# Pairwise attention on one Trainium2 core: the 28 second slots of a tile all on ScalarE, and the copies of the transposed probabilities split one to three

## The reference, cut to what matters

```python
def _L1_gnn_ref(feat, adj, W1, W2, a):
    mask = jnp.where(adj > 0, 0.0, NEG_INF)
    q = feat @ W1.T
    k = feat @ W2.T
    e = jax.nn.relu(q[:, None, :, :] + k[:, :, None, :])   # every pair of nodes, 64 features
    scores = jnp.einsum('bijd,d->bij', e, a)
    att = jax.nn.softmax(scores + mask, axis=-1)
    return att @ feat
```

## Time and profile before

| | us |
|---|---|
| median of 3 runs (12303.48 to 12307.22) | 12305.15 |
| the profiled execution | 12303.05 |
| its span, first to last instruction | 12301.3 |
| PE busy in the span | 11965.8 (97%) |
| DVE busy | 10281.1 (84%) |
| ACT busy | 9346.4 (76%) |
| L611, slots on ScalarE, 3328 of them | 6398.1 |
| L881, first slots on VectorE, 4096 of them | 5252.8 |
| L1359, matmuls of the slots, 61440 | 6739.6 |

### The profile page before, as it was taken

How to read it: one execution, slowest core, us unless ns; L and a number is a source line. 1 busy time by engine, 2 the same in 40 slices (tenths; PEclk the granted TensorE clock), 3 DMA queues, 4 the chain that set the end, 5 groups by cost and what they waited for, 6 DMA issues and landing times.

```text
span 12301.3 us, 239883 instructions
## 1 busy us (share of the span) xinstructions
PE 11965.8 (97%) x106113; PEld 5936.3 (48%) x106113; DVE 10281.1 (84%) x12373; ACT 9346.4 (76%) x7633; POOL 458.4 (4%) x636
## 2 busy tenths in 40 slices
PE   7999999999999999999999999999999999999999
PEld 3333853338433384333843348433484334843348
DVE  4999849998599975999759997599975999759997
ACT  3898739987499874988748887489874898749986
POOL 1000000000000000000000000000000000000000
PEclk9999999999999999999999999999999999999999
DMA  2000320003200031000310003100031000310003
GB/s 74 19 21 22 105 80 22 18 22 113 76 18 18 24 117 69 18 18 26 125 59 18 18 27 132 52 18 18 31 137 43 18 22 29 140 38 19 21 32 106
DMA packets 206087, 609.72 MB, mean 50 GB/s; under 512 B 45440, under 2 KB 137216, under 8 KB 139520
## 3 DMA queue, kind: packets, MB, share of 16 engines
q1 hardware_dynamic: 184176, 450.72, 10.5%
q0 software_dynamic: 20880, 143.66, 3.1%
HBM read 556.47 MB, written 8.39 MB: 46 GB/s over the span
## 4 chain that ended last, share of the span: by engine, by line
DVE 52%; PE 45%; issue 1%; ACT 0%; SPq 0%; DMA 0%; POOL 0%; DVEq 0%
DVE E L881 34%; PE ps L1339 10%; DVE E L889 9%; PE ps L1443 8%; PE ps L1359 7%; PE ps L1456 4%; PE ps L1516 4%; PE ps L1423 4%; PE ps L1372 4%; DVE T L904 2%; PE ps L1502 2%; DVE E L879 1%; DVE HW L915 1%; DVE adj_ring L896 1%; PE ps L1322 1%
## 5 line engine op out<-in xcount | busy, mean ns | idle before, releaser
L611 ACT ACTIVATE E<-QB,KBP 128x2048 f32<-128x2048 f32 x3328 | 6398.1, 1994 | 740.0 <-PE ps L1359 722.3
L1359 PE MATMUL ps<-E,s_win 128*32 128x512 f32 x61440 | 6739.6, 594 | 104.0 <-DVE E L889 60.5
L881 DVE TENSOR_SCALAR E<-QA,KLO,KHI 128x2048 f32<-128x2048 f32 x4096 | 5252.8, 1339 | 20.0 <-DVE nmin L904 17.8
L1359 PEld LDWEIGHTS ps<-E,s_win 128*32 128x32 f32 x61440 | 1975.5, 110 | 4667.3 <-issue 4182.8
L1013 DVE CUSTOM_DVE_ANT_0 T<-ps,adj_ring 128x2048 f32<-128x2048 f32 x512 | 1171.6, 2288 | 88.9 <-PE ps L1423 86.2
L889 DVE SCALAR_TENSOR_TENSOR E<-QB,KBN,E 128x2048 f32<-128x2048 f32 x512 | 1200.3, 2344 | 0.0
L643 ACT ACTIVATE T<-T,nmin 128x2048 f32<-128x2048 f32 x512 | 1028.8, 2009 | 215.5 <-DVE nmin L1013 215.4
L1443 PE MATMUL ps<-ident,T 128*128 128x128 f32 x8192 | 1098.7, 277 | 15.7 <-DVE HT L975 12.3
L1443 PEld LDWEIGHTS ps<-ident,T 128*128 128x128 f32 x8192 | 913.5, 141 | 198.9 <-ACT PT L523 71.1
L523 ACT ACTIVATE AGG<-ps 128x512 f32<-128x512 f32 x224 | 126.7, 596 | 1012.5 <-PE ps L1339 980.9
L1339 PE MATMUL ps<-adj_res,H 128*128 128x512 f32 x2048 | 889.5, 592 | 0.0
(11 more groups left out here) (147 smaller groups left out, 7706.3 us busy)
## 6 DMA issues: line engine op xcount, KB each, us to landing
adj_ring<-in_adj SPq DMA_DIRECT2D x384, 1024.0 KB, 5.0
adj_res<-in_adj POOLq DMA_DIRECT2D x128, 1024.0 KB, 6.4
qcur<-AGG SPq DMA_DIRECT2D x896, 16.0 KB, 2.7
qcur<-HT SPq DMA_DIRECT2D x896, 16.0 KB, 2.2
HW<-in_x POOLq DMA_DIRECT2D x9, 1024.0 KB, 6.5
X<-in_x SPq DMA_DIRECT2D x128, 64.0 KB, 1.9
out_x<-X SPq DMA_DIRECT2D x8, 1024.0 KB, 16.9
wq_r<-in_L_gnn_Wq SPq DMA_DIRECT2D x4, 64.0 KB, 2.3
```

The costliest lines, as they stand in the source:

```text
L611: last = nc.scalar.activation(E[:, e_slot(t, k) + g, :], QB[:, :], ACT.Relu, bias=KBP[:, col:col + 1])
L881: last = nc.vector.tensor_scalar(dst, QA[:, :], KLO[:, col:col + 1], KHI[:, col:col + 1], ALU.max, ALU.min)
L1359: last = mm(ps[QROWS * g:QROWS * (g + 1), 4 * u + c, :], win, E[:, s + g, c * CH:(c + 1) * CH], start=(k == 0), stop=(k == NS - 1), tile_p ...
```

## The change

ScalarE makes every second slot: per step 2, 2, 2, 2, 2, 1, 2, 2, 2, 1, 3, 1, 2, 2, 2 (28). VectorE makes none, which takes one slot from its step 1 and one from its step 10. In `evac1` ScalarE copies chunk 0 alone and VectorE chunks 1, 2 and 3.

```diff
-SCALAR_TWO = tuple(k for k in range(NS) if k != 1)
+ACT_CHUNKS = 1
...
     for row in zip(*[column_group(g) for g in range(4)]):
-        left = 2 if len(plan) in SCALAR_TWO else 1
         step = []
         for kind, m in row:
-            by_act = kind == "second" and left > 0
-            left -= by_act
-            step.append((kind, m, by_act))
+            step.append((kind, m, kind == "second"))
         plan.append(step)
...
             def evac1(T, u):
-                for g in range(2):
+                for g in range(ACT_CHUNKS):
                     act.wait_ge(pt1_ps, T * NC + g + 1)
...
-                    if kind == "second":
-                        last = nc.vector.tensor_scalar(dst, QB[:, :], KBN[:, col:col + 1], None, ALU.max)
-                    else:
-                        last = nc.vector.tensor_scalar(dst, QA[:, :], KLO[:, col:col + 1], KHI[:, col:col + 1], ALU.max, ALU.min)
+                    last = nc.vector.tensor_scalar(dst, QA[:, :], KLO[:, col:col + 1], KHI[:, col:col + 1], ALU.max, ALU.min)
...
             def evac1(T, u):
-                for g in range(2, 4):
+                for g in range(ACT_CHUNKS, NC):
                     dve.wait_ge(pt1_ps, T * NC + g + 1)
```

## The result

The changed kernel takes **12,362.4 us** (median of 4 runs, 12,358.5 to 12,363.8) against 12,305.2: a ratio of 1.0046, 95% interval 1.0029 to 1.0063. It is slower by 57 us. The profiled execution's span is 12,361.1 us against 12,301.3.

What follows compares the result with a forecast made beforehand. Order, not busy shares, was taken as the bound, with ScalarE already deciding step 4's start. Terms 6.8 + 0.5 - 0.36 + 0.12 = 7.1 us a batch, +57, gave 12,362 us (range 12,335 to 12,390).

Steps and rivals of the forecast that it cites:

- Step 4 waits for ScalarE: Before step 4 of an ordinary tile: TensorE waits 1.57 us for ScalarE, 1.43 more than before the change.
- The waits before steps 8 and 9 go: In ordinary tiles TensorE no longer waits for VectorE at these two steps: -0.81 us a tile.
- The third copy is covered: VectorE's added copy between steps 7 and 8 costs nothing under TensorE's wait for ScalarE; uncovered, 0.60 us a tile.
- Step 10's slot is free: Moving it costs zero: ScalarE's waits before step 13 hide it, VectorE's product wait grows from 1.28 to about 2.8.
- Tiles 0 and 1: First two tiles of a batch: step 4 of tile 1 +1.19 us, waits behind it -1.55, together -0.36.
- End of a batch's stage: At TensorE's last product, three copies start 0.48 us earlier and take 0.60 longer: +0.12 us.
- Tiles 5, 9, 13: Tiles with four more VectorE normalisations: 0.2 us stays before step 8, about +0.17 each, +0.5 a batch.
- Rival A: VectorE was the bound, so every wait vanishes: 20 us a batch faster, 12,145 us; chance 4%.
- Rival D: A 1.57 us wait in each tile lowers TensorE's clock afterwards: +204 us, 12,565; chance 2%.
- The sum: All terms of a batch's stage added: 7.1 us a batch, +57 us, 12,362 us.

Runs made afterwards that it cites:

- four copies: ScalarE copies all four chunks and VectorE none, slots as before, on the kernel before the change: 12,193.9 us.
- all three together: On the kernel before the change, ScalarE copies all four chunks and also makes step 10's slot, its exponential after step 4: 12,174.4 us.
- the copy alone: ScalarE copies chunk 0 and VectorE the other three, slots as before, on the kernel before the change: 12,373.5 us.
- the later exponential: The changed kernel with ScalarE's exponential after step 4 in place of step 3, same work: 12,332.9 us.
- the slots alone: Both slots (steps 1 and 10) go to ScalarE and the copies stay two and two, against the kernel before: 12,353.1 us.

## Why the prediction was right

- *Step 4 waits for ScalarE.* Forecast 1.57 us, found 1.58. That ScalarE already set step 4's start before, although the trace named VectorE, is borne out: between the runs with four copies and with all three together, 3.55 us from step 3 to step 4 become 3.43. These two differ in the exponential's place and in step 10's slot, which moves nothing in an ordinary tile when it goes alone. In the change, moving the exponential alone takes the whole 1.58 away.
- *The waits before steps 8 and 9 go.* They did, in the ordinary tiles, and the tile came to 59.00 as forecast (+0.61 for +0.62).
- *The third copy is covered.* It is, by TensorE's wait for ScalarE, and costs 0.60 a tile without it, as the run of the copy alone shows. In tiles 5, 9 and 13 nothing covers it: the pair of tiles 5 and 6 takes 119.28 with it and 118.66 without.
- *Step 10's slot is free.* It is in an ordinary tile, on both engines: ScalarE's 1.77 took it up and VectorE's wait for the product grew (2.73; 2.8 was forecast). ScalarE has a new wait of 0.56 before step 10 and 2.73 before step 13 where I had 2.8 to 3.5; neither is on the path.
- *Tiles 0 and 1.* ScalarE writes 36 slots without a wait from 1795.42 and step 4 of tile 1 comes 1869.63 - 1799.46 = 70.17 us into the stage, 1.17 later than before (1.19 forecast). Tile 2 begins 113.90 us in, before 114.33: -0.43 for -0.36.
- *End of a batch's stage.* From the end of the last tile's steps to TensorE's last product it is 2752.85 - 2743.29 = 9.56 us, before 2736.58 - 2727.18 = 9.40: +0.16 for +0.12.
- *Tiles 5, 9, 13: a term mis-sized.* Of the changed kernel, TensorE's steps 6 to 9 in tile 5 (timeline), then tiles 5 and 6 (window):

```profile
2114.54 7.07 PE L1353 MATMUL ps<-E,s_win 128*32 128x512 f32 x64
2121.85 7.41 PE L1353 MATMUL ps<-E,s_win 128*32 128x512 f32 x64 [0.23 <-DVE E L883]
```

```profile
2090.36:2209.64 119.28, 116.44 (x1065) 42.16 (x1061) 111.63 (x96) 112.45 (x65) 0.00 (x0) 1.00 0.06 19
```

  Step 8 waits 0.45 (2121.85 - 2114.54 - 6.86), not 0.2: VectorE was 0.6 early, not 0.8. The hand-over to its minimum takes 0.47 (step 14 ends at 1955.17 + 17.16 = 1972.33, the minimum starts at 1972.80), where I had used the 0.28 of ScalarE's slots; most of the 0.1 that the later exponential missed in every tile is the same. Tile 5 and the one behind it together take 119.28, before 118.40 (the same window there, below): +0.88 for the forecast's 0.17 + 0.62 = 0.79, 2 us over all 24.

```profile
2079.89:2198.29 118.40, 116.78 (x1064) 41.73 (x1060) 115.03 (x99) 106.39 (x62) 0.00 (x0) 1.00 0.05 19
```
- *Rival A, VectorE as the bound,* is refuted: the slots alone take 2.4 us a tile from it and lose 49 us. Its direction, not its size, comes out with the exponential after step 4: the slots alone then gain 43 us, where the rival had 160, and the full change is still slower than before (12,332.9).
- *Rival D, the clock,* was put at 2% and as a matter of every tile. It is none at 1.58 us of waiting, but it did happen behind tile 1's 2.34 in 2 of 8 batches, some 3.4 us of the profiled execution. The forecast had left this out: it put tile 1's step 4 1.19 us later but did not say how long TensorE then waits there.
- *The sum.* Batch 1, without a slow step 4, is 6.99 us longer in the stage, and 0.16 behind it, which makes 57.2 us in eight, for the 57 of the sum; with the slow steps the profiled spans differ by 59.8, the medians by 57.2. The mechanism and its main terms are right. That the median lands within 1 us of 12,362 is luck in part: the range was 12,335 to 12,390, and the clock's 3.4 us and the 2 us of tiles 5, 9 and 13 stood outside the sum.

## What to carry to other kernels

When three engines work in lock-step through a shallow ring of buffers, count the work of each between the last place where it waited and the place where it is waited for, not over the whole period: a slot cost 32 us or nothing, depending on which side of that wait it stood. The trace may name the engine whose instruction had long ended; compare end times with the start of the waiting one. Then move first what is only in the way (here the exponential, one step later) or goes ahead of a late engine's slots (the copies), before moving work by busy shares. The copies are shown for the kernel before (111 us with all four); the exponential was moved only together with other work, and no run has it alone on the kernel before.

## What was not expected of the hardware

Behind a wait of TensorE of 2.34 us its granted clock was lower in the next step in 7 of 8 batches of one kernel (the slots alone) and 2 of 8 of another (the change); each time the step took 5.13 us for 3.43. The wait was the same, but for one batch of the change, where it was 1.90 and the clock stayed. Waits of 1.3 to 1.6 us, 14 in every batch (tiles 2 to 15), had no low clock behind them in either kernel. Taking the wait away brought every batch back.

What decides between two equal waits is open; nothing was run for it. The traces hold one sign. The first step of a batch's stage runs at a low clock for a part of it, and its length varies. The nine batches with a slow step 4 are those whose first step took 4.72 to 4.99 us; in the six others with a wait of 2.34 it took 5.03 to 5.13. Two such first steps of the change, batches 2 and 1, counted from 0; the first of them has the slow step 4 behind it, the second has not:

```profile
3335.61:3340.57 4.96, 4.96 (x33) 1.41 (x37) 4.96 (x7) 4.96 (x3) 0.00 (x0) 0.69 0.02 3
1799.46:1804.49 5.03, 5.03 (x32) 1.41 (x36) 5.03 (x7) 5.03 (x3) 0.00 (x0) 0.68 0.01 3
```

That is a coincidence in fifteen batches, not a shown cause. A short first step alone does nothing: with tile 1's exponential moved, four batches had one of 4.73 to 4.94 us and no slow step 4.
